# Attention after a mixture-of-experts stage: who copies the query heads, how far ahead the next sequence is prepared, and where the last projection stands

## The reference, cut to what matters

```python
qkv = (x @ Wqkv.T + bqkv).reshape(B, S, 3, H, d)...          # H = 16 heads of 8
kb = kp[:, :, idx, :]                                        # each block of queries sees its neighbourhood
scores = einsum('bhncd,bhnld->bhncl', qc, kb) / sqrt(d)
scores = where(band, scores, -inf)
attn = softmax(scores)
o = einsum('bhncl,bhnld->bhncd', attn, vb)...
return o @ Wout.T + bout                                     # the projection
```

## Time and profile before

| what | value |
|---|---|
| time before, median of 3 runs | 1823.41 us (1822.92 to 1826.37) |
| the profiled execution: its own time, its span | 1829.28 us, 1827.5 us |
| busy over the span: PE, PEld, DVE, ACT, POOL | 1630.0, 1396.1, 1258.8, 1076.7, 1196.7 us |
| attention stage, first to last block start | 1333.0 to 1605.9 us |
| score matmuls L1445: busy, idle before them | 76.7 us, 38.3 us, of which 36.3 until ACT's head copies |

### The profile page before, as it was taken

The page is one execution under the profiler, slowest core; times in us unless marked ns, Lnnn a source line. Parts: engine busy times, 40 slices in busy tenths (PEclk is TensorE's granted clock), DMA queues, the critical chain, the costliest instruction groups (busy, mean ns, idle before and its releaser), DMA issues. The chain is left out here.

```text
span 1827.5 us, 40267 instructions
## 1 busy us (share of the span) xinstructions
PE 1630.0 (89%) x14217; PEld 1396.1 (76%) x14217; DVE 1258.8 (69%) x2948; ACT 1076.7 (59%) x1947; POOL 1196.7 (65%) x1191
## 2 busy tenths in 40 slices
PE   6999898999999989988687998999968888889998
PEld 6888777777778867876566897788857777778887
DVE  2359889788898887888989435544456877656443
ACT  3476766766667757666665545344357777743442
POOL 4238787786877867879898534466556576544663
PEclk9999999999999999998898999999979999989999
DMA  5023333333333323322232311111346665311113
GB/s 154 1 73 114 102 98 101 96 96 99 112 96 108 101 82 114 96 96 85 86 97 64 105 52 35 35 49 47 116 137 184 187 184 175 95 34 37 49 51 105
DMA packets 141089, 171.23 MB, mean 94 GB/s; under 512 B 32246, under 2 KB 76316, under 8 KB 140892
## 3 DMA queue, kind: packets, MB, share of 16 engines
q1 hardware_dynamic: 133852, 153.06, 27.9%
q0 software_dynamic: 7040, 15.60, 2.7%
HBM read 116.30 MB, written 52.30 MB: 92 GB/s over the span
## 5 line engine op out<-in xcount | busy, mean ns | idle before, releaser
L833 POOL TENSOR_TENSOR db<-du_m,bt 128x512 f32<-128x512 f32 x256 | 329.1, 1287 | 116.9 <-DVE bank L838 116.2
L838 DVE TENSOR_TENSOR_SCAN bank<-bank,db 128x512 f32<-128x512 f32 x256 | 312.7, 1221 | 18.2 <-ACT bank L823 17.6
L864 POOL TENSOR_TENSOR y_m<-y_m,ph 128x512 f32<-128x512 f32 x240 | 312.8, 1304 | 2.0 <-DVE ph L853 2.0
L823 ACT ACTIVATE bank<-dt_m,a_neg 128x512 f32<-128x512 f32 x256 | 176.3, 689 | 86.0 <-DVE ph L853 79.1
L853 DVE TENSOR_TENSOR ph<-bank,ct 128x512 f32<-128x512 f32 x240 | 166.0, 692 | 9.4 <-POOL y_m L864 1.0
L1368 POOL TENSOR_TENSOR s_a<-s_a,mx_a 128x768 f32<-128x768 f32 x64 | 94.0, 1469 | 65.1 <-DVE mx_a L1459 61.1
L1445 PE MATMUL bank<-kT_a,qd_a 128*128 128x96 f32 x512 | 76.7, 295 | 38.3 <-ACT qd_a L1269 36.3
L1445 PEld LDWEIGHTS bank<-kT_a,qd_a 128*128 128x128 f32 x512 | 67.2, 203 | 47.0 <-ACT qd_a L1269 40.4
L375 PEld LDWEIGHTS bank<-dn,hf1b 128*128 128x128 f32 x680 | 90.2, 194 | 16.2 <-DVE x_all L437 6.8
L375 PEld LDWEIGHTS bank<-dn,hf2b 128*128 128x128 f32 x680 | 90.1, 194 | 15.9 <-DVE x_all L437 8.3
L375 PEld LDWEIGHTS bank<-dn,hf0b 128*128 128x128 f32 x688 | 90.3, 193 | 12.0 <-DVE x_all L437 2.8
(11 more groups left out here) (474 smaller groups left out, 4723.9 us busy)
## 6 DMA issues: line engine op xcount, KB each, us to landing
bt<-bc_rows SPq DMA_DIRECT2D x128, 256.0 KB, 3.5
ct<-bc_rows SPq DMA_DIRECT2D x128, 256.0 KB, 3.4
sorted<-zero_row SPq DMA_DIRECT2D x64, 288.0 KB, 4.0
kT_a<-k_rows SPq DMA_DIRECT2D x32, 256.0 KB, 3.4
q_strips_a<-q_rows SPq DMA_DIRECT2D x32, 256.0 KB, 4.3
q_rows<-q_hi_a SPq DMA_DIRECT2D x16, 256.0 KB
q_rows<-q_lo_a SPq DMA_DIRECT2D x16, 256.0 KB
k_rows<-k_hi_a SPq DMA_DIRECT2D x16, 256.0 KB, 3.4
```

Source lines behind the costliest of these rows:

```text
L823: eng.activation(DH[J % 2][:], dt[s % 2][:, j % NH, :], ACT.Exp, scale=a_neg[:, j % NH, j // NH:j // NH + 1]).then_inc(da_done.sem)
L833: eng.tensor_tensor(db[J % RD][:], du[s % 2][:, j % NH, :], bt[N % RB][:], ALU.mult).then_inc(db_done.sem)
L838: eng.tensor_tensor_scan(DH[J % 2][:], DH[J % 2][:], db[J % RD][:], 0.0, ALU.mult, ALU.add).then_inc(hs_done.sem)
L864: eng.tensor_tensor(y[s % 2][:, j % NH, :], y[s % 2][:, j % NH, :], ph[J % RP][:], ALU.add).then_inc(ys_done.sem)
```

## The change

- **Heads.** ACT copies head 0 only, POOL heads 1, 2 and 3. Group n is now set one step sooner: POOL copies head 1 at step 2n - 6 and heads 2 and 3 at 2n - 5, ACT copies head 0 at step 2n - 5, directly behind the exp, ahead of `copy_out` and of the copies of the probabilities. In the stage before, head 0 is copied ahead of the last shared step, and three heads behind it.
- **Preparation one step sooner.** Statistics at k = 2, root at 3, norm at the end of 4, T at the end of 5, q at the start of 6, k at its end, SP's stores and the first strips at k = 7. v stays at k = 1. The projection of s - 1 moves from k = 5 to 4, `norms.mean` from 6 to 5, `norms.root` from 7 to 6.
- **The last projection** leaves the attention block. SP issues its load as the first thing in the last stage, PE runs it behind slot 1 there into bank HT[1], DVE adds it in slot 2 and then makes the norm statistics of sequence 7, POOL makes the root behind the first sequence's scatters, DVE the scale in slot 5. All 28 unread matmuls are gone.
- **The table.** At t = 62 ACT runs a GELU on one column, so that the table is loaded there.
- The tiles `zt` and `oT` are laid out ahead of the others.

```diff
-        q_set, q_set2 = S.count("a_queries_set", NG, (0, 1)), S.count("a_queries_set_pool", NG, (2, 3))
+        q_set, q_set2 = S.count("a_queries_set", NG, (0,)), S.count("a_queries_set_pool", NG, (1, 2, 3))
...
-                if k == (0 if s >= 1 else 1) and more:
-                    store_queries(eng, s + 1)
-                    store_keys(eng, s + 1)
-                    strips(eng, s + 1, 0)
+                ahead_of = s + 1 if k < GU - 1 else s + 2
+                if (t == 1 or t >= GU - 1 and k == GU - 1) and ahead_of < NSEQ:
+                    store_queries(eng, ahead_of)
+                    store_keys(eng, ahead_of)
+                    strips(eng, ahead_of, 0)
...
-            load_out(eng, NSEQ - 1)
...
         def pool(eng):
...
                 if t == 0:
-                    set_by_pool(eng, 2, 2, 2)
-                n, r = ((t + 5) // 2, 2) if t % 2 else (t // 2 + 2, 3)
+                    set_by_pool(eng, 2, (1, 2, 3), 2)
+                n = (t + 6) // 2
                 if n < NG:
-                    set_by_pool(eng, n, r, t + 2)
-                if k == 4 and s + 2 < NSEQ:
+                    set_by_pool(eng, n, (2, 3) if t % 2 else (1,), t + 2)
+                if k == 3 and s + 2 < NSEQ:
                     norm_root(eng, s + 2)
-                if k == GU - 1 and 1 <= s < NSEQ:
+                if k == GU - 2 and 1 <= s < NSEQ:
                     norms.root(eng, s - 1)
...
-            names = ... else {(6, 2): "T", (7, 0): "q", (7, 2): "k", (1, 0): "v"}
+            names = ... else {(5, 2): "T", (6, 0): "q", (6, 2): "k", (1, 0): "v"}
...
-            return (s,) if t % GU == 5 and 0 <= s < NSEQ - 1 else ()
+            return (s,) if t % GU == 4 and 0 <= s < NSEQ - 1 else ()
...
-                if t == NU:
-                    warm(eng, BT[0], K["up_hi"][0], 4)
-            warm(eng, BT[0], K["up_hi"][0], 20)
-            project_pe(eng, NSEQ - 1)
-            warm(eng, BT[0], K["up_hi"][0], 4)
...
         def act(eng):
...
+                n = (t + 6) // 2
...
+                if t % 2 and n < NG:
+                    set_queries(eng, eng.copy, n, (0,))
                 if t >= 2:
                     copy_out(eng, t - 2)
...
-                    if place == 2 and k == 5 and s + 2 < NSEQ:
+                    if place == 2 and k == 4 and s + 2 < NSEQ:
                         norm_out(eng, s + 2)
...
-                n, r = ((t + 5) // 2, 0) if t % 2 else (t // 2 + 2, 1)
-                if n < NG:
-                    set_queries(eng, eng.copy, n, (r,))
                 if t == NU - 2:
+                    eng.activation(table[:], C["one"][:], ACT.Gelu)
                     next(norms_next)
...
-            project_dve(eng, NSEQ - 1)
+        closing.update(load_out=load_out, project_pe=project_pe, project_dve=project_dve, projected=(r_done.sem, r_done.at(NSEQ - 1)))
...
@@ ffn1 @@
+            if closing:
+                closing["load_out"](eng, NSEQ - 1)
...
+                if v == 1 and closing:
+                    closing["project_pe"](eng, NSEQ - 1, HT[1].psum)
+                    HT[1].free = closing["projected"]
...
-                    opening["set_queries"](eng, eng.copy, 0, (0, 1))
+                    opening["set_queries"](eng, eng.copy, 0, (0,))
...
-                opening["set_queries"](eng, eng.copy, 0, (2, 3))
+                opening["set_queries"](eng, eng.copy, 0, (1, 2, 3))
...
-                if v == -2:
+                if v == -2 and first:
                     norms.mean(eng, NSEQ - 1)
-                if v == 1:
+                if v == (1 if first else 5):
                     norms.scale(eng, NSEQ - 1)
...
+                if v == 2 and closing:
+                    closing["project_dve"](eng, NSEQ - 1, HT[1].psum)
+                    eng.wait_ge(*closing["projected"])
+                    norms.mean(eng, NSEQ - 1)
```

More of the change, by code:

```diff
@@ L1070, in front, with attention @@
             block.tensor(pe)
-def attention(nc, S, C, bank, K, a, host):
+def attention(nc, S, C, bank, K, a, host, closing):
     NB = SEQ // QB
@@ L1098, in attention @@
         q_hi, q_lo, k_hi, k_lo = (sb(n, [P, SEQ], F32R) for n in ("q_hi", "q_lo", "k_hi", "k_lo"))
-        band = sb("band", [P, KW])
+        band, table = sb("band", [P, KW]), sb("table", [P, 1])
         v_tok = xn
@@ L1311, in attention @@
         sb("groups", [P, RS * SEQ + RQ * HG * SEQ + RK * PADDED])
+        zt, oT = [sb(f"zt{r}", [HD * UB, P]) for r in range(RZ)], sb("oT", [P, 2, SEQ // 2])
         vb = two("vb", [KW, NB + 1, D])
@@ L1315, in attention @@
         pT, rc = two("pT", [KW, UB, P]), two("rc", [P, UB])
-        o1, oT = two("o1", [P, HD, UB]), sb("oT", [P, 2, SEQ // 2])
-        zt = [sb(f"zt{r}", [HD * UB, P]) for r in range(RZ)]
+        o1 = two("o1", [P, HD, UB])
         def store_out(eng, u):
@@ L1791, in pool @@
                 K["pool"](eng, tri_f)
-            else:
-                norms.root(eng, NSEQ - 1)
             if opening:
@@ L1796, in pool @@
             for s in range(NSEQ):
+                if s == 1 and not first:
+                    norms.root(eng, NSEQ - 1)
                 eng.wait_ge(pd.sem, pd.at(s, "slot"))
@@ L2270, in program @@
         front(nc, S, C, bank, sb, a["L0_attn_x"], a, f0, K, f1, M["sorted"])
-        last = ffn1(nc, S, C, bank, K, M, "_f1b", out, None, True)
-        stage = attention(nc, S, C, bank, K, a, last)
+        closing = {}
+        last = ffn1(nc, S, C, bank, K, M, "_f1b", out, None, True, closing)
+        stage = attention(nc, S, C, bank, K, a, last, closing)
         every(ffn1(nc, S, C, bank, K, M, "_f1", None, next(stage)))
```

34 lines of the change are left out of this document (17 added, 17 removed).

## The result

The change makes the kernel faster by 0.64%: ratio 0.9936, 95% interval 0.9913 to 0.9959, with medians of 1829.6 us before (8 runs, 1818.9 to 1836.0) and 1816.6 after (8 runs, 1811.3 to 1821.3). So the gain is 9.5 to 12 us where 19.8 were forecast. The forecast's 1803.6 us started from 1823.41, the median of three runs; eight runs put the kernel before at 1829.6. The profiled execution after took 1818.85 us (span 1817.0) against 1829.28.

A forecast was written before the change was run, and what follows sets the result against it. No engine was full; waits for ACT's head copies and a transfer loop through SP as long as the 30.5 us period were taken as the bound. Terms -0.6 - 9.5 + 0.5 - 5.0 - 6.3 + 0.7 + 0.4 = -19.8 gave 1803.6 us, range 1793 to 1817.

The forecast's parts named there:

- the step sooner: Attention periods: preparation moved a step earlier makes SP's transfer loop 29.4 us; five periods -13.3, -9.5 after the clock's share.
- Opening seam: Start of attention: ACT copies one head fewer ahead of the last shared step, -0.6 us (bounds -1.2 to 0).
- Heads: Attention: four copies per sequence go from ACT to POOL; if nothing else came, DVE's 3.0 us wait goes, 27.5 per sequence.
- The sign that was set against it: ACT waiting over 10 us in all for strips, or DVE 3 us per sequence for scores, would show the heads step wrong.
- Half of the clock's loss kept: Five attention periods: the slow clock costs 7.6 us before; half, 3.8, was assumed to stay.
- First sequence: First attention sequence: strips are late already, queues stand for them and POOL has one more copy, +0.5 us (0 to +1.6).
- Behind the last preparation: End of attention (1536 to 1600): no transfer loop is left, DVE's waits for scores go, -5.0 us (-2.5 to -5.7).
- rival C: Strips asked for sooner arrive late in every sequence, PE stands and slow clock follows: +16.3, near 1839.7 us; chance 0.08.
- Closing seam: Attention to last stage: the last stage starts sooner, -6.3 us; table load at t = 62 +0.7; last stage itself +0.4.
- the +3 end: Last stage: upper end of the +/-3 us allowed for the clock, if without unread matmuls it begins at half clock.
- B: Attention: no transfer bound, all DVE waits go, periods near 27.5 us, time near 1789.6; chance 0.15.
- D: Attention: the loop gives nothing back, five periods stay at 160.3 us, -7.8 in all, 1815.6; chance 0.22.

The follow-up runs named there:

- e17: Kernel before run against itself, nothing changed: ratio 0.9994 (0.9969 to 1.0019).
- e18: Kernel before with the new tile layout alone, no instruction added or moved, a repeat of e14 beside e17: ratio 1.0055 to the kernel before.
- e14: Kernel before with the new tile layout alone, no instruction added or moved: ratio 1.0045 to the kernel before.
- e13: Changed kernel without the closing seam and the new layout, so heads and preparation a step sooner on the old layout: ratio 0.9958 to the kernel before.
- e5: Changed kernel measured again as a yardstick: ratio 0.9948 (0.9919 to 0.9977) to the kernel before.
- e7: Changed kernel with v's store issued on SP ahead of the load for the projection and one output store: ratio 0.9918 to the kernel before.
- e11: Changed kernel with v's store first, v's load a step later, strips of groups 1 and 3 sooner, projection at the start of k = 5: 0.9916 to the kernel before.
- e12: e11 plus a tile of its own for v and the second sequence's first head group copied a step later: ratio 0.9890 to the kernel before.
- e1: Kernel before with the closing seam alone changed, its new tile layout included: ratio 1.0012 (0.9985 to 1.0039) to the kernel before.
- e6: Changed kernel plus 260 unread matmuls put where PE stood: ratio 0.9982 to the kernel before.
- e15: e1 plus 12 unread matmuls behind the last units of the attention stage: ratio 1.0007 to the kernel before.
- e16: e12 plus 12 unread matmuls at the end of the attention stage: ratio 0.9841 to the kernel before, on a slower chip than e12.

## Why the prediction was wrong, step by step

Two steps failed: the layout, which had no term, and the length of the loop through SP, which "the step sooner" put at 29.4 us. The measured median, 1816.6, lies at the upper end of the range (1793 to 1817).

The most useful cut of the attention stage is by exponentials, one per unit: the starts of those of units 0, 16, 48 and 63 in the timelines.

| us between units | 0-16 | 16-48 | 48-63 |
|---|---|---|---|
| before, e17 | 69.9, 68.6 | 128.8, 127.3 | 51.2, 51.2 |
| new layout alone: e18, e14 | 74.8, 73.9 | 129.7, 129.3 | 55.1, 54.6 |
| heads and step, old layout: e13 | 76.7 | 120.1 | 46.6 |
| changed, e5 | 71.4, 72.0 | 123.2, 123.2 | 52.5, 47.9 |
| e7 / e11 / e12 | 70.0 / 72.6 / 72.8 | 119.6 / 118.0 / 116.9 | 46.4 / 47.1 / 48.8 |

**The layout: no term at all, +8 to +10.** This is the first step that failed. The prediction gave the new order of tiles no price, not even a bound. Put beside the forecast, -19.8 + 8 to 10 = -10 to -12, and -9.5 to -12 was measured. That agreement is luck in part: the heads and the step fell short on the old layout too (e13), and by ratios e13, the seam's -5.2 and the layout make only -3 to -5. With intervals of 3 to 5 us to either side of each ratio, whether the parts add stays open.

**Opening seam, -0.6:** not shown. From the opening's q projection to the first scores it is 22.49 before and 21.71 after, but the kernel before has 21.60 in e17, and e1, with the old heads, 21.43.

**Heads:** right in mechanism. ACT's head waits are gone, and what is late next is SP. The sign that was set against it came up all the same: ACT waits 10.2 us for strips (10.7 in e5) where over 10 was to mean that the step is wrong, while DVE's wait for scores, 15.2 us over eight sequences, stays under its 3 per sequence. "Half of the clock's loss kept" was not borne out: half speed in this stage took 42.6 and 39.5 us in the two profiles of the kernel before, 61.3 and 44.3 in those of the changed one.

**The step sooner, 29.4 us per period:** the second step that failed. The mechanism was right (the norm starts at the landing of v's store, to 0.01 us, three times in the profile after and in all five periods of e13), the term 22.0 + 0.6 + 6.8 was too short. In e13, on the old layout, it measured 23.5 + 7.1, periods of 30.8. The 22.0 was read from the fastest period, where v's store landed 2.9 us behind its issue; in e13 it takes 3.7 to 4.8. Five periods sum to 153.8 in e13, 154.4 and 153.0 in the changed kernel, against 160.3 and 157.3: -3 to -7 where -9.5 was forecast, and no loss to the layout in them. The cut by exponentials gives e13 more, -8.0 for four sequences against the mean of before and e17, and the changed kernel -4.9; the two cuts differ by where they begin, so neither fixes the size to better than 3 us. What the prediction left out besides is the projection: it named the load among the loop's members but did not ask what stands behind a PE that waits for it. The loop's second half, 6.8 us from norm to q_lo, is 6.6 to 7.6 in the other periods after, and 10.1 in the period shown above.

**First sequence, +0.5 (0 to +1.6):** too small. Against the mean of before and e17, 69.3, units 0 to 16 take 2.2 and 2.7 more; e13 takes 7.5 more, on the old layout. The new layout alone takes 4.6 and 5.5 more (e14, e18). The in-order stall was named; half speed behind it was not priced.

**Behind the last preparation, -5.0:** -3.3 in e5 and -4.6 in e13, but +1.3 in the profile after. There the last sequence's strips came late, and POOL stood 5.26 and ACT 3.48 for them; PE stood 1.88 for the heads, and 10.2 us at half speed followed. This is rival C's mechanism, once, not seven times.

**Closing seam, -6.3 + 0.7 + 0.4:** -6.2 from the last copy_out to the last stage, as forecast. The last stage itself is longer by 1.4 us than in the profile before, by 3.2 and 3.9 than in those of e18 and e17, where the forecast had +0.4 with bounds of 3. From the last copy_out to the end that leaves -2 to -5 of the -5.9. GELU was to start 1.28 us sooner without its table load; it starts 0.14 sooner (2.95 behind the stage's first instruction, before 3.09), and 1.4 sooner only where the stage begins at full speed (1.69 in e6, e15 and e16). That the seam pays by the ratios is shown only by difference: e1 against e14 is -0.33%, e15 against e14 -0.38%, near the -5.2, each with an uncertainty about as large as itself.

The Trainium skill (TensorE: Matmul & The Clock Gate, Part 1), by which the slow clock is the default and activity releases it, was weighed there for the +3 end. The traces agree with it at the seam: without unread matmuls the last stage begins at half speed in all twelve profiles, with 12 of them in neither of two. No ratio shows a cost of that, e15 brings nothing over e1; and inside attention e6 gets the clock back and no time.

**Rivals.** B's periods of 27.5 exist, in e12, once v has its own tile and SP's order is changed. D's figure (-7.8) is nearest to the measured one. Its reason, that the loop gives nothing back, is half right: five periods gave back 3 to 7 us where the forecast had 9.5 and D nothing.

## What to carry to other kernels

Price a change of tile layout like a change of code: run the old kernel with the new layout alone. A candidate, not tried here: one-column tiles behind those that transfers write to, or padded to 256 bytes. A loop that closes through a queue is as long as its transfers take on average, not as in its fastest turn. When several consumers hang on one queue that issues in order, removing one wait only names the next; count the whole queue's order, first what the longest chain needs (here v's store), and put nothing that waits for a landing between two requests that could go out. And a kernel whose runs spread by 1% needs the old kernel against itself as its yardstick.

## What the runs showed of the hardware

- Tiles that start 32 bytes behind a 256-byte boundary went with 512-byte packets of 40 instead of 32 ns on average (the order of two tiles had changed too).
- Pauses of PE of about 2 us were followed by half speed: in the profile after, 10.2 us behind a wait of 2.08 us for the projection's load, 10.2 us behind one of 1.88 for the heads, and 10.2 us at the seam, where PE does nothing for 1.6 us between the blocks. With 12 unread matmuls ahead of the seam (e15, e16) there was none at the seam.
- The amount differs between executions of one kernel. Half speed in the attention stage took 42.6 and 39.5 us in the kernel before, whose PE idles 40.3 and 38.6 us there, mostly 1.3 at a time; 61.3 and 44.3 in the changed one, with 29.3 and 33.4 us idle in fewer pauses.
- The kernel before took 1820 to 1848 us in its runs on four of the chips, and the spread follows the mean granted clock (in 15 of the 18 kernels here the correlation is -0.68 to -0.98).
